# The one-hot tables of a routing step with a block's 16 picks innermost: fp16 comparisons on VectorE, stepped columns on TensorE

## The reference, cut to what matters

```python
scores = jax.nn.sigmoid(logits)                       # 2048 tokens x 16 experts
...
topk_idx = jax.lax.top_k(masked, TOP_K)[1]            # 4 experts for each token
topk_weight = jnp.take_along_axis(scores, topk_idx, axis=1)
...
routed = jnp.einsum('ntf,nhf,tn->th', act, down_w, weight_matrix)
out = routed + _swiglu(hidden, sh_gate_w, sh_up_w, sh_down_w)
```

## Time and profile before

| | us |
|---|---|
| median of 3 runs | 794.3 |
| lowest, highest | 794.25, 794.47 |
| the profiled execution | 791.16 |
| its span | 789.4 |
| TensorE busy in it (matmuls) | 713.2 |
| VectorE busy | 507.8 |
| ScalarE busy | 340.5 |
| GpSimd busy | 384.9 |

### The profile page before, as it was taken

How to read it: one execution, slowest core, us unless ns; L and a number is a source line. 1 busy time by engine, 2 the same in 40 slices (tenths; PEclk the granted TensorE clock), 3 DMA queues, 4 the chain that set the end, 5 groups by cost and what they waited for, 6 DMA issues and landing times.

```text
span 789.4 us, 13948 instructions
## 1 busy us (share of the span) xinstructions
PE 713.2 (90%) x4849; PEld 635.7 (81%) x4849; DVE 507.8 (64%) x1296; ACT 340.5 (43%) x698; POOL 384.9 (49%) x450
## 2 busy tenths in 40 slices
PE   4899988959999991778999999999999999999995
PEld 2444557848999980668899999999999999999995
DVE  3999997975666645676566566575574675653422
ACT  2563633245666652265444253444434533443221
POOL 5876956047766605544264363543652643322322
PEclk9999998988999995679999999999999999999999
DMA  8675505946866764424021020010020110000000
GB/s 246 196 166 133 142 27 125 210 108 179 245 195 197 163 146 126 155 71 130 1 61 34 8 61 28 14 59 22 29 63 5 41 41 1 2 15 1 14 1 14
DMA packets 44595, 68.61 MB, mean 87 GB/s; under 512 B 7376, under 2 KB 32240, under 8 KB 44528
## 3 DMA queue, kind: packets, MB, share of 16 engines
q0 software_dynamic: 10080, 28.72, 16.5%
q1 hardware_dynamic: 34352, 38.97, 15.5%
q10 hardware_dynamic: 96, 0.04, 0.0%
HBM read 50.77 MB, written 14.84 MB: 83 GB/s over the span
## 4 chain that ended last, share of the span: by engine, by line
PE 53%; POOL 3%; DVE 2%; ACT 2%; issue 2%; POOLq 0%; DVEq 0%
PE psum L1457 20%; PE psum L1442 10%; PE psum L1489 9%; PE psum L1502 4%; PE psum L1475 3%; PE psum L1538 2%; PE psum L1515 2%; PE psum L1528 2%; POOL rows_back L1728 1%; PE psum L1556 1%; ACT lora_w_hi L1618 1%; DVE lora_w_lo L1819 0%; PE psum L1546 0%; PE psum L1569 0%; PE psum L1576 0%
## 5 line engine op out<-in xcount | busy, mean ns | idle before, releaser
L1953 DVE TENSOR_TENSOR hid<-hid,psum 128x256 f32<-128x256 f32 x112 | 47.0, 420 | 152.2 <-ACT hid L1625 152.2
L1457 PE MATMUL psum<-am_hi,lora_w_hi 128*128 128x256 f32 x448 | 127.4, 284 | 2.0 <-DVE am_lo L1948 2.0
L1748 POOL TENSOR_TENSOR hid<-hid,ratio_sb 128x256 f32<-128x256 f32 x56 | 41.5, 741 | 176.9 <-DVE hid L1953 176.7
L1457 PE MATMUL psum<-am_hi,lora_w_lo 128*128 128x256 f32 x448 | 127.4, 284 | 0.0
L1457 PE MATMUL psum<-am_lo,lora_w_hi 128*128 128x256 f32 x448 | 127.2, 284 | 0.0
L1625 ACT ACTIVATE hid<-psum 128x256 f32<-128x256 f32 x112 | 42.9, 384 | 183.3 <-PE psum L1457 183.2
L1033 POOL DMA_INDIRECT rows_in<-y_scratch,slot_token x80 | 76.0, 950 | 30.9 <-issue 26.5
L1457 PEld LDWEIGHTS psum<-am_hi,lora_w_hi 128*128 128x128 f32 x448 | 86.2, 192 | 2.2 <-POOL am_lo L1759 2.1
L1457 PEld LDWEIGHTS psum<-am_hi,lora_w_lo 128*128 128x128 f32 x448 | 86.3, 193 | 0.0
L1457 PEld LDWEIGHTS psum<-am_lo,lora_w_hi 128*128 128x128 f32 x448 | 86.2, 192 | 0.0
L1728 POOL DMA_INDIRECT rows_back<-slots_scratch,comb_idx x64 | 66.8, 1043 | 39.2 <-POOLq L697 23.7
(11 more groups left out here) (250 smaller groups left out, 2050.2 us busy)
## 6 DMA issues: line engine op xcount, KB each, us to landing
slots_scratch<-y_out SPq DMA_DIRECT2D x40, 256.0 KB, 3.3
stage<-in_moe_weights SPq DMA_DIRECT2D x18, 384.0 KB, 3.8
moe_w_lo<-in_moe_weights POOLq DMA_DIRECT2D x18, 384.0 KB, 7.1
lora_stage_early<-in_lora_weights SPq DMA_DIRECT2D x16, 384.0 KB, 3.5
x_sb<-in_x SPq DMA_DIRECT2D x4, 512.0 KB, 6.3
ctx_t<-in_ctx_t SPq DMA_DIRECT2D x4, 512.0 KB, 7.3
y_scratch<-y SPq DMA_DIRECT2D x8, 256.0 KB, 2.2
x_sb<-shared_out POOLq DMA_DIRECT2D x4, 512.0 KB, 5.3
```

The lines of the kernel that those rows point to most:

```text
L1457: last = nc.tensor.matmul(x_banks[F % 2][:, w * GT:(w + 1) * GT], wp, ap, start=False, stop=(half == 1 and k == 2), skip_group_check=True)
L1748: nc.gpsimd.tensor_tensor(f[:, F % 2, 1, :], f[:, F % 2, 1, :], ratio_sb[:, F // FB % 2, :], ALU.mult)\
L1953: nc.vector.tensor_tensor(f[:, F % 2, k, :], f[:, F % 2, k, :], x_banks[F % 2][:, GT:2 * GT], ALU.mult)\
```

## The change

Both tables get another order: block, then lane or tile, and the block's 16 picks innermost. `lane_hot` becomes [128, 4 blocks, 128 lanes, 16 picks] and `tile_hot` [128, 4, 80 tiles, 16]. In a comparison the picks are then the innermost dimension of all three operands: `lane_of` and `tile_of` are kept with four picks a token tile instead of eight columns, so that a block's 16 are adjacent, and are repeated over the lanes or tiles; the constant numbers are written out 16 times each by iota (`lanes` 128 x 16, `tile_ids` 80 x 16; before 128 and 80). These wider constants lie where `rows_in` lies later. A matmul of the table reads its 128 weights and its 80 moving columns with a step of 16 elements (32 bytes). The scaling by token numbers handles the same 320 elements as 80 runs of four. Order of the queues, semaphores and counts of instructions stay.

```diff
@@ tables @@
-    with nc.sbuf_tensor("lane_hot", [P, N_PICKS, P], FP16) as lane_hot:
+    with nc.sbuf_tensor("lane_hot", [P, HOT_BLOCKS, P, HOT_PICKS], FP16) as lane_hot:
-    tile_hot, reached = sb("tile_hot", [P, N_PICKS, ROUTED_TILES], FP16), sb("reached", [P, ROUTED_TILES, E])
+    tile_hot, reached = sb("tile_hot", [P, HOT_BLOCKS, ROUTED_TILES, HOT_PICKS], FP16), sb("reached", [P, ROUTED_TILES, E])
-    tile_of, lane_of = (sb(n, [P, T, 8], FP16) for n in ("tile_of", "lane_of"))
+    tile_of, lane_of = (sb(n, [P, T, TOP_EXPERTS], FP16) for n in ("tile_of", "lane_of"))
-    lanes, tile_ids = sb("lanes", [P, P], FP16), sb("tile_ids", [P, ROUTED_TILES], FP16)
+    with ExitStack() as place:
+        lanes = place.enter_context(nc.sbuf_tensor("lanes", [P, P, HOT_PICKS], FP16))
+        tile_ids = place.enter_context(nc.sbuf_tensor("tile_ids", [P, ROUTED_TILES, HOT_PICKS], FP16))
     rows_in = sb("rows_in", [P, ROW_SLOTS, ROW])
@@ helpers @@
+        def picks_of(v, block, width):
+            return v[:, block * HOT_TILES:(block + 1) * HOT_TILES, :].rearrange("p t k -> p (t k)").unsqueeze(1)\
+                .broadcast_to([P, width, HOT_PICKS])
+
+        def of_tile(u):
+            first = u % HOT_TILES * TOP_EXPERTS
+            return tile_hot[:, u // HOT_TILES, :, first:first + TOP_EXPERTS]
@@ slot_table, TensorE @@
-                    last = nc.tensor.matmul(table_bank[:, 0:ROUTED_TILES], lane_hot[:, n, :], tile_hot[:, n, :],
-                                            start=(n == 0), stop=(n == N_PICKS - 1))
+                    pick = n % HOT_PICKS
+                    last = nc.tensor.matmul(table_bank[:, 0:ROUTED_TILES], lane_hot[:, block, :, pick],
+                                            tile_hot[:, block, :, pick], start=(n == 0), stop=(n == N_PICKS - 1))
@@ token_numbers, ScalarE (and the four of block 3 on VectorE alike) @@
-                    nc.scalar.activation(tile_hot[:, rows, :], tile_hot[:, rows, :], ACT.Copy,
-                                         scale=token_ids[:, u:u + 1]).then_inc(hot_ready, 1)
+                    nc.scalar.activation(of_tile(u), of_tile(u), ACT.Copy, scale=token_ids[:, u:u + 1])\
+                      .then_inc(hot_ready, 1)
@@ iotas, GpSimd @@
-                    (tile_nums, 0, [[1, ROUTED_TILES]], 0), (tile_ids, 0, [[1, ROUTED_TILES]], 0),
-                    (lanes, 1, [[1, P]], 0)):
+                    (tile_nums, 0, [[1, ROUTED_TILES]], 0)):
...
+            for out, base, width in ((tile_ids, 0, ROUTED_TILES), (lanes, 1, P)):
+                last = nc.gpsimd.iota(out[:, :, :], pattern=[[1, width], [0, HOT_PICKS]], base=base, channel_multiplier=0,
@@ comparisons, VectorE @@
-                nc.vector.tensor_tensor(hot_rows(lane_hot, block), ids(lanes, P), spread(lane_of, block, P),
+                nc.vector.tensor_tensor(lane_hot[:, block, :, :], lanes[:, :, :], picks_of(lane_of, block, P),
-                nc.vector.tensor_tensor(hot_rows(tile_hot, block), ids(tile_ids, ROUTED_TILES),
-                                        spread(tile_of, block, ROUTED_TILES), ALU.is_equal).then_inc(tile_hit, 1)
+                nc.vector.tensor_tensor(tile_hot[:, block, :, :], tile_ids[:, :, :],
+                                        picks_of(tile_of, block, ROUTED_TILES), ALU.is_equal).then_inc(tile_hit, 1)
```

More of the change, by code:

```diff
@@ L67 @@
 HOT_BLOCKS = TILES // HOT_TILES
+HOT_PICKS = HOT_TILES * TOP_EXPERTS
 LANE_ORDER = (0, 1, 2, 3)
@@ L815, in slot_table @@
                 pe.wait_ge(lane_hit, LANE_ORDER.index(block) + 1)
-                for n in range(block * HOT_TILES * TOP_EXPERTS, (block + 1) * HOT_TILES * TOP_EXPERTS):
+                for n in range(block * HOT_PICKS, (block + 1) * HOT_PICKS):
                     if n % TOP_EXPERTS == 0 and block < HOT_BLOCKS - 1:
@@ L933, in token_numbers @@
                 for u in range(block * HOT_TILES, (block + 1) * HOT_TILES):
-                    rows = slice(u * TOP_EXPERTS, (u + 1) * TOP_EXPERTS)
-                    nc.scalar.activation(tile_hot[:, rows, :], tile_hot[:, rows, :], ACT.Copy,
-                                         scale=token_ids[:, u:u + 1]).then_inc(hot_ready, 1)
+                    nc.scalar.activation(of_tile(u), of_tile(u), ACT.Copy, scale=token_ids[:, u:u + 1])\
+                      .then_inc(hot_ready, 1)
             nc.scalar.activation(scores[:, :, :], banks[7][:, 0:T * E].rearrange("p (t e) -> p t e", e=E),
@@ L1013, in _ @@
                     (thresholds, 0, [[P, T]], 0), (expert_ids, 0, [[1, E]], 0), (token_ids, 0, [[P, T]], 1),
-                    (tile_nums, 0, [[1, ROUTED_TILES]], 0), (tile_ids, 0, [[1, ROUTED_TILES]], 0),
-                    (lanes, 1, [[1, P]], 0)):
-                last = nc.gpsimd.iota(out[:, :], pattern=pattern, base=base, channel_multiplier=partition,
+                    (tile_nums, 0, [[1, ROUTED_TILES]], 0)):
+                nc.gpsimd.iota(out[:, :], pattern=pattern, base=base, channel_multiplier=partition,
+                               allow_small_or_imprecise_dtypes=True)
+            for out, base, width in ((tile_ids, 0, ROUTED_TILES), (lanes, 1, P)):
+                last = nc.gpsimd.iota(out[:, :, :], pattern=[[1, width], [0, HOT_PICKS]], base=base, channel_multiplier=0,
                                       allow_small_or_imprecise_dtypes=True)
@@ L1152, in tiles_and_lanes @@
                 dve_step(nc.vector.tensor_scalar_add(tile_at[:, :, :], tile_at[:, :, :], ROUNDING))
-                dve_step(nc.vector.tensor_scalar_add(tile_of[:, :, :], tile_at[:, :, :], -ROUNDING))
+                dve_step(nc.vector.tensor_scalar_add(tile_of[:, :, :], tile_at[:, :, 0:TOP_EXPERTS], -ROUNDING))
                 dve_step(nc.vector.scalar_tensor_tensor(lane_of[:, :, :], tile_of[:, :, :], -float(P),
-                                                        slot_best[:, :, :], ALU.mult, ALU.add))
+                                                        slot_best[:, :, 0:TOP_EXPERTS], ALU.mult, ALU.add))
             def lane_hots(block):
-                nc.vector.tensor_tensor(hot_rows(lane_hot, block), ids(lanes, P), spread(lane_of, block, P),
+                nc.vector.tensor_tensor(lane_hot[:, block, :, :], lanes[:, :, :], picks_of(lane_of, block, P),
                                         ALU.is_equal).then_inc(lane_hit, 1)
             def tile_hots(block):
-                nc.vector.tensor_tensor(hot_rows(tile_hot, block), ids(tile_ids, ROUTED_TILES),
-                                        spread(tile_of, block, ROUTED_TILES), ALU.is_equal).then_inc(tile_hit, 1)
+                nc.vector.tensor_tensor(tile_hot[:, block, :, :], tile_ids[:, :, :],
+                                        picks_of(tile_of, block, ROUTED_TILES), ALU.is_equal).then_inc(tile_hit, 1)
                 if block < HOT_BLOCKS - 1:
@@ L1167, in tile_hots @@
                 for u in range(block * HOT_TILES, (block + 1) * HOT_TILES):
-                    rows = slice(u * TOP_EXPERTS, (u + 1) * TOP_EXPERTS)
-                    nc.vector.tensor_scalar_mul(tile_hot[:, rows, :], tile_hot[:, rows, :], token_ids[:, u:u + 1])\
+                    nc.vector.tensor_scalar_mul(of_tile(u), of_tile(u), token_ids[:, u:u + 1])\
                       .then_inc(last_hot_ready, 1)
```

## The result

The changed kernel takes 800.0 us (median of 4 runs, 799.41 to 801.31) where the kernel before takes 794.27 (4 runs, 793.14 to 794.47). The ratio is 1.008, with an interval of 1.0065 to 1.0095: slower. I had said 795.3 us, with a range up to 799.3. The time lies above the range.

The account below looks back on a forecast made before the run. TensorE was taken to bound the routed stage, so its start moves the end. Comparisons -0, table +0.95 and iotas +0 took the profiled 791.16 to 792.1 us; the median, 3.1 higher, gave 795.3, range 793.7 to 799.3.

Parts of the forecast that it names:

- the formula behind it: GpSimd's first gather comes late by 0.063 us for each ns above 51 ns a table pair, nothing below.
- I take the ratio, 36 x 1.83 = 66 ns: TensorE's stepped table reads slow by VectorE's ratio, from 36 to 66 ns a pair, making the table 0.95 us late.
- The nearest bound I had: Upper bound for a TensorE table pair: 0.86 ns added to each of 128 weights, 146 ns, 6.0 us late.
- dear step: Rival: TensorE's stepped table reads cost over 76 ns a pair; 797.7 us at 105 ns, 800.3 at 146; chance 0.30.
- The two iotas: GpSimd's wide constants take 2.8 us more together, covered by spare time in the queues; cost 0.
- the rival that they slow VectorE: Long GpSimd iotas slow eight two-input VectorE operations, up to 2.2 us: 796.5, or 797.5 us with the table; chance 0.05.
- The comparisons: VectorE's eight fall to 1.24 and 0.83 us each, 6.8 us in all, hidden by ScalarE and GpSimd; gain 0.
- The scaling: ScalarE's twelve and VectorE's four operations by token numbers, now in runs of four, cost 0; bounds 0 and 0.8 us.
- a rival in which a shorter idle stretch gives time back: TensorE's clock holds because a longer table leaves less idle time; 2.4 us come back, 792.8 us; chance 0.05.

Follow-up runs that it names:

- c: b with tile_hot put back to adjacent order, so that only the table's weights are read at a 32-byte step; one run, 793.56 us.
- e: The changed kernel with four picks innermost instead of sixteen, a step of 8 bytes; ratio 1.0023 to the kernel before.
- d: b with lane_hot put back to adjacent order, so that only the moving columns are read at a 32-byte step; one run, 797.71 us.
- b: The changed kernel with narrow iotas, the constants widened later by two ScalarE copies; ratio 1.0058 to the kernel before.
- n: The changed kernel with the copy of g_mask written as a two-input maximum of equal inputs, on the third chip; 827.64 us, ratio 1.0121 to the kernel before.
- m: The changed kernel as it is, run once more on the third chip; 829.13 us, ratio 1.0126 to the kernel before.
- a: The kernel before with only the two wide iotas added, written and never read; ratio 1.0041 to the kernel before.
- i: The kernel before, old layout, with queues reordered so TensorE makes the whole table before the last two shared_down; ratio 1.001, repeat 0.9981.
- j: The reordered queues of i with the layout of c (only weights stepped); ratio 0.9985 to the kernel before, repeat 0.9974.

## Why the prediction was wrong

**What bounds it, and the formula behind it: right.** The lateness was to be 0.063 us for each ns above 51 ns a pair. At the measured 60, 75, 146 and 152 ns that gives 0.6, 1.5, 6.0 and 6.4 us; c, e, d and b measured 0.65, 1.63, 5.99 and 6.44. TensorE's table, cast and gather follow each other as the timeline of before said. That the late start also reaches the end is shown by the changed kernel: 9.23 us more to the first gather, 9.60 from the small iota to the end of the span.

**The step that failed: "I take the ratio, 36 x 1.83 = 66 ns".** It measured 152. TensorE's pair is not slowed by VectorE's ratio. Its stepped columns alone bring it to 146 ns, its stepped weights alone to 60, and both together to 152, so the weights are read for the most part beside the columns. Nor do stepped weights add nothing, as a sentence of the prediction had it: alone they add 24 ns. The nearest bound I had was 146 ns, and I had worked it out for the wrong half: 0.86 ns for each of the 128 weights, where it is about 1.4 ns (110 / 80) on top for each of the 80 columns. The rival "dear step" was right, with 0.30; it alone would have priced this kernel at 800.3 us. That this is nearly the median is luck: the table costs 6.4 of 9.2 us in the trace, and before's profiled execution was the fast one.

**The second step that failed: "*The two iotas.* Cost 0".** They are 2.47 and 1.59 us long, 4.06 in all (3.6 more than the narrow two, not 2.8), and on GpSimd's queue they are covered as I said: the first weight transfer went at 131.31 and nothing behind it was late. But I gave the rival that they slow VectorE 0.05, looking only at operations with two inputs, and priced it by the select (0.28 us each). The copy, with one input, was in the same stretch, and it is held for the rest of the iota. That plus the clock is 2.68 us by n against m; with b's 6.44 it makes 9.12 of the 9.23 us.

**The comparisons: right.** 1222 and 819 ns for 1.24 and 0.83, and hidden. The trace shows it: ScalarE's twelve still start when ScalarE is free, and VectorE idles from 167.4 to 177.03.

**The scaling: right.** ScalarE's twelve take 5.54 us, as before, in runs of four.

**The clock: the other way.** I had a rival in which a shorter idle stretch gives time back. TensorE worked without a gap from 163.44 to 176.92, and its granted clock still fell to half at about 173.4; routed matmuls ran at half until about 190.5, where before the full clock came at 181.9. The two windows in which it changes:

```profile
173.00:174.00 1.00, 1.00 (x9) 0.96 (x8) 0.00 (x0) 0.00 (x0) 0.00 (x0) 0.70 1.01 197
190.00:191.00 1.00, 1.00 (x9) 1.00 (x8) 0.59 (x2) 0.00 (x0) 0.70 (x2) 0.77 0.24 87
```

Inside the table the clock changes nothing, as the last 48 pairs keep one pitch across the fall. What the later rise costs behind it was not separated.

**What stays open.** The medians differ by 5.7 us, the parts alone by 3.5 (a) and 4.0 (b), with intervals of 1.2 and 2.1 us to either side, and the traces by 8.5. Of that 8.5, 2.8 us is where the two profiled executions stand to their medians. Which stretch of before varies so was not traced. Nor is it known what ScalarE waits for on the second and third chip, or why the clock fell within a table without gaps.

## What to carry to other kernels

A layout that makes one engine's access contiguous makes another's stepped: price both, by the engine that ends last, and try the step by itself before the rest is built around it. A faster operation under a cover wins nothing; in i and j the lane comparisons mattered as soon as the queues exposed them, at the first gather more than in the whole. When a long instruction is added on GpSimd, look at each VectorE operation beside it, above all copies, and at who waits behind them.

## What the runs showed of the hardware

- TensorE reading fp16 at a step, both operands: a pair of 128 weights and 80 columns takes 36 ns adjacent, 75 at 8 bytes, 149 at 16, 152 at 32. At 32 bytes the columns alone make it 146, the weights alone 60. The Trainium skill (SBUF — State Buffer, Specifications) says that two hits a 16-byte line are needed for full bandwidth. By it 8 bytes, two columns a line, should cost nothing; e's 75 ns say otherwise, and the measurement decides. That 16 and 32 bytes cost the same agrees with it.
- A copy (one input, one output) stood still on VectorE for the rest of an iota (0.20 us became 0.49, 1.35, 1.36 and 1.70), while operations with two inputs, and a reduce, took their 0.22 or 0.23 beside it. The Trainium skill (SBUF — State Buffer, Who interferes with whom) has this, for a copy in a mode of two ports, as an exclusive lock on a pair of ports shared with GpSimd; an operation with two inputs contends only with a GpSimd operation that reads. An iota reads nothing, and the trace agrees. I had not brought it to bear on the copy.
- Iota over two dimensions costs more than the 0.9 ns an element that I took from the narrow ones, and the more the shorter the inner run: 2048 elements in runs of 16 take 2.47 us (1.2 ns each), 1024 in runs of eight 1.93 (1.9), 512 in runs of four 1.19 (2.3).
- The clock that had risen about a microsecond before fell back after idle waits of TensorE of 1.77, 2.08 and 2.28 us, in the three profiles where the copy was held over 1.3 us (m, changed kernel, a). It stayed full where this wait was 1.23 us or less, and also in n, where the wait was 2.69 us but the clock had been full since 120 us. So the length of the wait alone does not decide it.
